# A two-layer gated network on one core: the first stage's normalisation moved to ScalarE, merge units issued in pairs, and one batch's projections started in another PSUM bank

## The chip, the core and the metric

The kernel runs on one core of a Trainium2 chip. The metric is the device time of one execution in microseconds (us), as the median of several runs; lower is better. All tensors are float32 unless a part says bf16. The engines are TensorE (PE in the profile; PEld is its weight load), VectorE (DVE), ScalarE (ACT), GpSimd (POOL) and SyncE (SP, which here only issues DMAs). Each engine works through its own list in order; between engines there are only counted semaphores.

## What is computed

The input `x` is 32 batches of 112 rows by 256 columns, `ctx` is 32 batches of 375 rows by 512 columns. Four blocks are added to `x` one after the other, each with a gate `tanh(g)` and each on a layer-normalised `x`:

```
x = x + tanh(g_xattn[0]) * L0_xattn(layernorm(x), ctx, mask)   # stage 1
x = x + tanh(g_ffn[0])   * L0_ffn(layernorm(x))                 # stage 2
x = x + tanh(g_xattn[1]) * L1_xattn(layernorm(x), ctx)          # stage 3
x = x + tanh(g_ffn[1])   * L1_ffn(layernorm(x))                 # stage 4
```

Stage 1: `x` is RMS-normalised and multiplied by `W_in` plus `b_in`; to it comes a decaying sum over the first rows of the RMS-normalised `ctx`, with weights `exp(-dt * distance)` where the distance comes from a running count over the mask. Stage 2: a hidden layer gives each batch eight gate values; the weights of both matrices of an MLP (256 to 1024 to 256) are merged per batch as `W + sum_e g[b, e] * TW[e]`; the MLP is then run with them. Stage 3: attention with 16 heads of 16 columns over the 375 rows of `ctx` and the 112 rows of `x`, with products of float32 quality made out of bf16 parts. Stage 4: a gated column MLP with a softmax, and a last layer norm.

## The kernel before

**Stage 1** (`stage1`, lines 192 to 478). SP loads the mask, constants, four copies of the `b_in` row (line 260) and then `x` and `ctx` in eight groups of four batches (lines 263, 264). DVE turns the mask into indices and compares them with a row of numbers in one instruction for all batches (`hit`, line 337: output bf16, inputs float32). PE counts the hits (96 products with one column each, line 438), sums them up (line 443) and spreads the result over 32 products (line 447) into eight banks. DVE evacuates the distances in two halves (line 351) and scales them (`distances`, line 300, the first half before the batches, the second during batch 9). ACT squares the rows of `ctx` (line 398). For each half of 16 batches DVE and ACT make the inverse roots together (`inverses`: ACT's root at line 404, DVE's steps at lines 101 to 105).

Then come the 32 batches, in rings of four buffers. For batch b: DVE normalises (`front`, line 361, issued two batches ahead); PE transposes (`turn`, line 458); ACT takes one exponential (line 417) and evacuates the transposed x (line 419); POOL scales the `ctx` rows (line 279) and multiplies them by `g_init` (line 282); PE makes four products with `w_in` (line 468) and two with the exponentials and the rows of `u` (line 471; a float32 product is two instructions); DVE adds the result to the residual (line 367) and takes its statistics (lines 370 and 383). Between the batches DVE also takes the statistics of later groups of `x` (lines 291 and 294).

**Stage 2** (`stage2`, lines 481 to 840). DVE forms the variances of all 32 batches, ACT their roots, DVE the inverses (lines 101 to 105), and only then does `norm` (line 110) give PE something to transpose (line 750). After the gates come eight chunks of the hidden width. A merge unit is four pairs of products with 64 rows of contraction each (`merge_unit`, line 792), after which DVE adds the base weights in two instructions (line 641). A chunk has two phases. In the first, for each of eight groups of four batches: one merge unit for the second matrix, then 16 instructions of the first product (line 815; all 128 rows). In the second, for each two pairs of batches: one merge unit for the first matrix of the next chunk, then 8 instructions of the second product (line 832; 128 rows), whose result DVE adds to the residual (`added`, line 660). Merge results go to two pairs of banks in turn, so unit n waits for DVE's work on unit n-2; the second product's results go to two banks in turn, so pair p waits for `added` of p-2. The last chunk has no second-phase units.

```
for g in range(NG):                     # PE, first phase of a chunk, before
    merge2(c, g)
    ... 16 products of group g ...
```

POOL meanwhile splits the keys of `ctx` into three bf16 parts and stores them to DRAM.

**Stage 3** (`stage3`). A schedule written out by hand over turns -4 to 33 sets the order on each engine; `at(b, operation)` issues the part of batch b that belongs to a turn. A batch is prepared two turns before its scores: `norm` (DVE), `turn_x` (PE, line 1232), `evacuate_x` (ACT, line 1031), `queries_keys` (PE, line 1239), `first_part` (ACT, line 1039), `split` (DVE, line 1159), the parts (POOL, lines 978 to 988), four groups of transposes `turn_parts` (PE, line 1265), evacuated by ACT (keys, line 1054) and DVE (queries, line 1182), and `later_queries` (ACT, line 1064). All of these use one bank, PREP. Then `scores_by_query` (PE, line 1283) and `maximum` (DVE, line 1169) find the row maxima; `scores` (line 1309) and `outputs` (line 1323) follow. For the first batches there is extra work: POOL clears the pads of three rings of buffers (lines 958 to 962) and puts head markers into them (`place_heads`, line 995); ACT does this for the first ring (line 1024); DVE takes the statistics of batches 8 to 31 in three blocks of eight (`late_statistics`, lines 1132 and 1135), the last one between the two evacuations of the first batch's queries.

## Time and profile before

| | |
|---|---|
| median of 3 runs | 1434.84 us (1430.89 to 1436.14) |
| the profiled execution's own time | 1429.99 us |
| its span from the first to the last instruction | 1428.2 us, 32631 instructions |
| mean granted TensorE clock | 0.969 of full speed |
| PE, DVE, ACT, POOL busy | 1324.7, 981.9, 665.4, 558.0 us |

The stages in this execution: stage 1 ends at about 121 us, stage 2 at about 560 us, stage 3 at about 1150 us, stage 4 at 1428 us. How to read the rows below: a time of start and a duration are in microseconds; "x16" is the number of like instructions taken together; in brackets stands how long the engine had been idle before, and what ended that. Matmuls overlap each other's ends, so the distance of two starts tells their pace and the duration does not. The granted clock is 1.00 at 2.4 GHz and 0.50 at 1.2 GHz.

### The profile page before, as it was taken

The numbers are of one execution on the slowest core, as the hardware profiler recorded it, in microseconds if no ns is written. First come the engines' busy times: TensorE is split into PE (matmuls) and PEld (weight loads), VectorE is DVE, ScalarE is ACT, GpSimd is POOL, SyncE is SP. The second block draws the span as 40 slices with busy tenths as digits, with TensorE's granted clock in tenths as the row PEclk, the third lists the DMA queues.
The fourth block names the chain that finished last, engine by engine and source line by source line (L and its number), as shares of the span: only waits on it lengthen the run. The fifth ranks groups of instructions, "written<-read, shape, count | busy, mean of one in ns | idle before, by whom it ended". The sixth has DMA issues, their size and how long they took to land. (4 is left out here: it accounts for less than half of the span.)

```text
span 1428.2 us, 32631 instructions
## 1 busy us (share of the span) xinstructions
PE 1324.7 (93%) x12672; PEld 923.5 (65%) x12672; DVE 981.9 (69%) x1646; ACT 665.4 (47%) x1436; POOL 558.0 (39%) x831
## 2 busy tenths in 40 slices
PE   3687999999999997699999999999999799999997
PEld 2455577777777775367766676766776574555555
DVE  6767656765676567588888888888887554445444
ACT  4433322112112212478878787787877554122221
POOL 0566888888882002533232332323331183000000
PEclk9989999999999999599999999999999799999998
DMA  8404354545451202955566655566552000000000
GB/s 230 107 1 137 98 170 133 161 137 164 137 162 64 66 1 46 174 88 89 89 104 104 100 89 89 98 103 101 95 89 34 2 1 0 14 14 13 26 13 26
DMA packets 92773, 120.25 MB, mean 84 GB/s; under 512 B 7414, under 2 KB 78899, under 8 KB 90348
## 3 DMA queue, kind: packets, MB, share of 16 engines
q1 hardware_dynamic: 83436, 87.82, 30.9%
q0 software_dynamic: 9216, 30.73, 7.7%
q8 instruction: 86, 1.41, 0.4%
q14 instruction: 35, 0.29, 0.1%
HBM read 96.42 MB, written 22.10 MB: 83 GB/s over the span
## 5 line engine op out<-in xcount | busy, mean ns | idle before, releaser
L1169 DVE TENSOR_REDUCE s_neg_max<-banks 112x3 bf16<-112x1461 f32 (+1 forms) x192 | 290.2, 1511 | 45.2 <-PE banks L1283 44.6
L1085 ACT ACTIVATE s_prob<-banks 128x448 f32<-128x448 f32 x512 | 272.4, 544 | 91.8 <-PE banks L1309 76.9
L641 DVE TENSOR_TENSOR s_m<-banks,s_base 128x512 f32<-128x512 f32 x256 | 164.7, 686 | 128.4 <-PE banks L792 128.3
L1309 PE MATMUL banks<-s_q_t,s_k_t 112*128 112x112 bf16 x2048 | 186.6, 215 | 1.1 <-ACT s_prob L1085 1.0
L1309 PEld LDWEIGHTS banks<-s_q_t,s_k_t 112*128 112x128 bf16 x2048 | 124.3, 98 | 72.8 <-issue 50.0
L792 PE MATMUL banks<-s_gate_sel,s_tw 64*128 64x256 f32 x1024 | 146.7, 406 | 1.0 <-DVE s_m L641 0.8
L815 PEld LDWEIGHTS banks<-s_x_t,s_m 128*128 128x128 f32 x1024 | 119.1, 191 | 21.4 <-issue 20.9
L815 PE MATMUL banks<-s_x_t,s_m 128*128 128x112 f32 x1024 | 130.5, 280 | 0.1
L832 PE MATMUL banks<-s_m,s_act_t 128*112 128x256 f32 x512 | 128.5, 388 | 0.6
L1323 PE MATMUL banks<-s_prob,s_v 128*32 128x112 f32 (+1 forms) x4096 | 125.7, 263 | 0.7 <-ACT s_prob L1085 0.7
L732 ACT ACTIVATE s_act_t<-banks,s_bias 128x112 f32<-128x112 f32 x256 | 69.6, 354 | 98.9 <-PE banks L815 98.8
L1801 PE MATMUL banks<-s_proj,s_weighted 128*112 128x256 f32 x512 | 115.4, 380 | 0.0
L792 PEld LDWEIGHTS banks<-s_gate_sel,s_tw 64*128 64x128 f32 x1024 | 89.4, 188 | 36.9 <-issue 20.6
L1801 PEld LDWEIGHTS banks<-s_proj,s_weighted 128*112 128x112 f32 x512 | 90.3, 177 | 28.3 <-issue 10.5
L832 PEld LDWEIGHTS banks<-s_m,s_act_t 128*112 128x112 f32 x512 | 83.4, 176 | 34.9 <-issue 13.9
L732 ACT ACT_TABLE_LOAD x8 | 10.3, 1283 | 202.1 <-PE banks L815 202.1
L1323 PEld LDWEIGHTS banks<-s_prob,s_v 128*32 128x32 f32 (+1 forms) x4096 | 94.6, 110 | 12.4 <-ACT s_prob L1085 1.0
L660 DVE SCALAR_TENSOR_TENSOR x_res<-banks,gates,x_res 112x512 f32<-112x512 f32 x128 | 93.3, 746 | 5.0 <-PE banks L832 4.3
L978 POOL CAST s_qk<-s_rest 112x512 bf16<-112x512 f32 x32 | 19.6, 613 | 176.5 <-DVE s_rest L1159 176.5
L968 POOL COPY s_v<-s_v_raw 128x768 f32<-128x768 f32 x32 | 26.3, 822 | 154.2 <-PE banks L1323 154.2
L1795 PE MATMUL banks<-s_x_t,s_w_cols 128*128 x192 | 85.0, 565 | 0.0
L1283 PE MATMUL banks<-s_k_t,s_q_t 32*112 32x487 bf16 x192 | 79.7, 415 | 4.9 <-DVE s_neg_max L1169 3.7
(270 smaller groups left out, 2311.6 us busy)
## 6 DMA issues: line engine op xcount, KB each, us to landing
k_parts<-s_k_split POOLq DMA_DIRECT2D x64, 281.2 KB, 3.7
s_k_t<-k_parts SPq DMA_DIRECT2D x32, 562.5 KB, 8.0
s_tw<-in_tw SPq DMA_DIRECT2D x16, 1024.0 KB, 5.0
s_k_raw<-in_ctx_k POOLq DMA_DIRECT2D x64, 187.5 KB, 3.8
s_k_t<-k_parts SPq DMA_DIRECT2D x32, 375.0 KB, 5.4
s_v_raw<-in_ctx SPq DMA_DIRECT2D x32, 256.0 KB
s_src<-in_ctx SPq DMA_DIRECT2D x8, 896.0 KB, 15.4
s_k_t<-k_parts SPq DMA_DIRECT2D x32, 187.5 KB, 9.2
```

Source lines behind the costliest of these rows:

```text
L641: nc.vector.tensor_tensor(dst[:, :, :, rows_], got, base[:, :, rows_].unsqueeze(2).broadcast_to([P, 2, B, HR]), ALU.add).then_inc(S["merge ...
L660: nc.vector.scalar_tensor_tensor(out=w.x_res[:, 2 * p:2 * p + 2, :], in0=w.bank(6 + p % 2, T).rearrange("t (b d) -> t b d", b=2), scalar=w ...
L732: last = nc.scalar.activation(act_t[:, b, :], w.bank(4 + g % 2)[:, r * T:(r + 1) * T], ACT.Gelu_apprx_tanh, bias=bias1[:, c, b, :])
L792: last = nc.tensor.matmul(w.bank(2 * (n[1] % 2) + half)[:, m * B * HR:(m + 1) * B * HR], rows_(m)[tile], sel[tile], start=True, stop=True)
L815: last = nc.tensor.matmul(w.bank(4 + g % 2)[:, r * T:(r + 1) * T], m1[:, kk, b, :], x_t[:, kk, b * T:(b + 1) * T], start=(kk == 0), stop=( ...
L832: last = nc.tensor.matmul(y, act_t[:, b, :], m2[:, b, :], start=not first, stop=True)
L1085: nc.scalar.activation(prob[t % 2][:, c, :], w.bank(SCORE + n % SRING, P, TILE), ACT.Exp, scale=DH ** -0.5).then_inc(S["exp_done"], 1)
L1169: nc.vector.tensor_reduce(neg_max[half][:, ROWS + first:ROWS + end, 0], w.banks[0:T, MAX:MAX + end - first, 0:NKEY], AX.X, ALU.max, negate ...
L1309: last = nc.tensor.matmul(w.bank(SCORE + n % SRING)[:, s * T:(s + 1) * T], k_t[k][0:ROWS_MAX, h, c * P:(c + 1) * P], q_t[k][0:ROWS_MAX, h, :],
L1323: last = nc.tensor.matmul(w.banks[s * SLOT:(s + 1) * SLOT, OUT, t * T:(t + 1) * T], v[k][0:K_OF[c], c, t * HS + s, :], prob[t % 2][0:K_OF[ ...
L1795: last = nc.tensor.matmul(w.bank(j % 2, P, GT), w_cols[:, kk, j * P:(j + 1) * P], x_t[:, kk, bass.ds(g * GT, GT)], start=(kk == 0), stop=( ...
L1801: last = nc.tensor.matmul(w.bank(4 + r, T, D), weighted[k][:, j, r * T:(r + 1) * T], proj[:, j, :], start=(j == 0), stop=(j == J4 - 1))
```

## The change

In stage 1 the normalisation goes from DVE (`tensor_scalar`) to ACT (`Identity` with a scale and a bias per row, the bias being `-mean * inverse`). The `hit` comparison is done in bf16 and in four quarters, each awaited by PE on its own. The inverse roots are made in quarters of eight batches instead of halves, so three of four now fall between batches. The second half's distances are evacuated by ACT; the exponentials are taken in place for four batches at once before batch 0 (first half) and before batch 2 (second half). POOL multiplies the `ctx` rows by `g_init` in place and scales the exponentials instead of the rows, in groups of four batches. The `b_in` rows come with one DMA as a 113th row of `src`. PE runs two batches ahead with `turn`. The inverse roots that stage 2 needs for batches 0 to 23 are made at the end of stage 1 (`next_roots`).

```diff
-                nc.vector.tensor_tensor(
-                    hit[:], iota[0:CHUNK, 0:T]....broadcast_to([CHUNK, NQ * B, T]),
-                    idx_t[:]....broadcast_to([CHUNK, NQ * B, T]), ALU.is_equal).then_inc(S["hit_done"], 1)
+                for q in range(Q):
+                    at = slice(q * QB, (q + 1) * QB)
+                    nc.vector.tensor_tensor(
+                        hit[:, :, at, :], iota16[0:CHUNK]....broadcast_to([CHUNK, NQ, QB, T]),
+                        idx_t[:, :, at].unsqueeze(3).broadcast_to([CHUNK, NQ, QB, T]), ALU.is_equal).then_inc(S["hit_done"], 1)
...
+                inverses(0)
+                evacuate_distances()
                 distances(0)
-                inverses(0)
...
+                wait(dve, "evac1", 1)
+                distances(1)
                 for b in range(B):
-                    if b == HB - 2:
-                        inverses(1)
-                    if b + 2 < B:
-                        front(b + 2)
                     last = back(b)
...
+                    if b < 3:
+                        chain.link(x_statistics(QB + 3 * b, min(QB + 3 * b + 3, HB)))
+                    elif b < 11:
+                        chain.link(x_statistics(HB + b - 3, HB + b - 2))
+                    elif b < 19:
+                        chain.link(x_statistics(HB + b - 3, HB + b - 2))
+                    if b in (2, 11, 19):
+                        inverses((b + 6) // 8)
+                    if b == 26:
+                        next_roots()
```

ScalarE's list of stage 1 after the change, after the squares of batches 0 to 7 and their root:

```diff
+                for b in range(QB, QB + GB):
+                    square(b)
+                for b in range(3):
+                    front(b)
+                wait(act, "init_done", 2)
+                wait(act, "spread", 2)
+                wait(act, "rows_done", 2)
+                nc.scalar.activation(expo[0:T, HB * T:B * T]..., w.banks[0:T, HG:NG, 0:GT],
+                                     ACT.Identity, bias=offset[0:T]).then_inc(S["evac1"], 1)
+                exps(0)
+                for b in range(2):
+                    evacuate_x(b)
+                front(3)
+                for b in range(QB + GB, HB):
+                    square(b)
+                exps(1)
+                for b in range(2, B):
+                    if b == 4:
                         roots(1)
+                    if b == 13:
+                        roots(2)
+                    if b == 21:
+                        roots(3)
+                    if b == 28:
+                        ... root for stage 2 ...
+                    evacuate_x(b)
+                    if b + 2 < B:
+                        front(b + 2)
+                    if 4 <= b < 20:
+                        square(HB + b - 4)
```

PE and POOL of stage 1:

```diff
-                    wait(pe, "m_done", b + 1)
-                    wait(pe, "u_done", b + 1)
-                    nc.tensor.matmul(y, m_scan[0:T + 1, r, :], u[0:T + 1, r, :], start=False, stop=True)\
+                    wait(pe, "scaled", b // GB + 1)
+                    wait(pe, "u_done", b // GB + 1)
+                    nc.tensor.matmul(y, expo[0:T + 1, b * T:(b + 1) * T], src[0:T + 1, b, 0:D], start=False, stop=True)\
...
                 turn(0)
+                turn(1)
+                wait(pe, "evac1", 1)
+                pe.wait_ge(bias_in, 16)
                 for b in range(B):
-                    if b + 1 < B:
-                        turn(b + 1)
+                    if b + 2 < B:
+                        turn(b + 2)
                     product(b)
```

In stage 2 two merge units follow each other in both phases, and `norm(0)` and `norm(1)` come before the roots of the last eight batches:

```diff
                     for g in range(NG):
-                        merge2(c, g)
+                        if g % 2 == 0:
+                            merge2(c, g)
+                            merge2(c, g + 1)
...
                     for p in range(PAIRS):
-                        if p % 2 == 0 and not final:
+                        if p % 4 == 0 and not final:
                             merge1(c + 1, p // 2)
+                            merge1(c + 1, p // 2 + 1)
...
-                    for p in range(PAIRS):
-                        if p % 2 == 0:
-                            merged1(c + 1, p // 2)
+                    for p in range(0, PAIRS, 4):
+                        merged1(c + 1, p // 2)
                         added(c, p)
+                        added(c, p + 1)
+                        merged1(c + 1, p // 2 + 1)
+                        added(c, p + 2)
+                        added(c, p + 3)
```

In stage 3 batch 1 is transposed and projected in the bank OUT before the first batch's parts are transposed; POOL clears the second and third ring later; ACT places the first ring's heads in two halves; DVE takes the late statistics of 16 batches in one block after the first `split`:

```diff
+        def prep(b):
+            return OUT if b == 1 else PREP
...
+                    if b == 0:
+                        clear(1)
                     if b < 2:
                         place_heads(b + 1)
+                    if b == 0:
+                        clear(2)
...
                     if b == 0:
-                        place_heads()
+                        evacuate_x(1)
+                        place_heads(0)
...
                     if b == 0:
-                        late_statistics(2 * EARLY, 3 * EARLY)
+                        late_statistics(2 * EARLY, B)
+                        variances(EARLY, B)
...
                 def turn_parts(b, n):
 
+                    if (b, n) == (0, 0):
+                        turn_x(1)
+                        for kk in range(KD):
+                            queries_keys(1, kk)
...
                         if b < RING:
-                            pe.wait_ge(rows_ready[k], 2)
+                            pe.wait_ge(rows_ready[k], 2 if k else 3)
...
                         wait(pe, "v_done", b + 1)
+                        if b == 0:
+                            wait(pe, "rest_done", 2)
```

## Rows read from the trace of the kernel before

**Rows 1.** Window of stage 1: length, PE, PEld, DVE, ACT, POOL busy, clock, DMA, GB/s:

```profile
62.00:77.00 15.00, 11.97 (x45) 8.68 (x43) 10.68 (x37) 6.52 (x24) 7.85 (x10) 0.77 0.00 1
```

**Rows 2.** Timeline, the head of stage 1 and one bf16 copy of stage 2:

```profile
12.16 11.36 DVE L337 TENSOR_TENSOR s_hit<-s_iota,s_idx_t 125x10752 bf16<-125x10752 f32 x1
23.58 9.12 PE L438 MATMUL banks<-s_ones,s_hit 125*112 125x1 bf16 x96 [13.88 <-DVE s_hit L337]
...
36.92 4.20 DVE L351 TENSOR_SCALAR s_expo<-banks,s_iota 112x1792 f32<-112x1792 f32 x2 [0.17 <-PE banks L447]
...
46.53 2.05 PE L468 MATMUL banks<-s_w_in,s_x_t 128*112 128x256 f32 x4
...
134.28 2.08 DVE L614 COPY s_batch_of<-s_ident 96x3584 bf16<-96x3584 bf16 x1
```

**Rows 3.** Timeline of PE, the start of one batch and of the next:

```profile
97.59 0.36 PE L458 MATMUL banks<-ident,s_xn 112*128 112x112 f32 x2
...
99.08 0.37 PE L458 MATMUL banks<-ident,s_xn 112*128 112x112 f32 x2
```

**Rows 4.** Groups of instructions by form, 0 to 125 us (busy us, mean ns | idle before):

```profile
L282 POOL TENSOR_TENSOR s_u<-s_src,s_g_init 112x256 f32<-112x256 f32 x32 | 25.1, 785 | 2.7
L398 ACT ACTIVATE s_squares<-s_src 112x512 f32<-112x512 f32 x32 | 19.8, 619 | 14.2 <-DMA s_src<-in_ctx 14.2
L361 DVE TENSOR_SCALAR s_xn<-x_res,mean_var,s_inv 112x256 f32<-112x256 f32 x32 | 16.5, 521 | 0.2
L370 DVE BATCH_NORM_STATS2 s_stats<-x_res 112x6 f32<-112x256 f32 x32 | 13.7, 427 | 1.1
L419 ACT ACTIVATE s_x_t<-banks 128x224 f32<-128x224 f32 x32 | 11.4, 356 | 40.3 <-PE banks L458 40.3
L404 ACT ACT_TABLE_LOAD x2 | 2.6, 1283 | 0.0
```

**Rows 5.** Timeline, the last work of stage 1 and PE's first of stage 2:

```profile
121.08 0.38 DVE L383 BATCH_NORM_AGGREGATE mean_var<-s_stats 112x2 f32<-112x6 f32 x4
...
126.18 3.22 PE L750 MATMUL banks<-ident,s_act_t 112*128 112x112 f32 x16 [6.06 <-DVE s_act_t L110]
```

**Rows 6.** Timeline of PE in a first phase; shorter windows show parts of the same runs:

```profile
279.71 2.04 PE L815 MATMUL banks<-s_x_t,s_m 128*128 128x112 f32 x16
281.68 1.13 PE L792 MATMUL banks<-s_gate_sel,s_tw 64*128 64x256 f32 x8
282.74 2.04 PE L815 MATMUL banks<-s_x_t,s_m 128*128 128x112 f32 x16
...
280.13 1.61 PE L815 MATMUL banks<-s_x_t,s_m 128*128 128x112 f32 x13
...
282.21 0.60 PE L792 MATMUL banks<-s_gate_sel,s_tw 64*128 64x256 f32 x4
...
282.43 0.38 PE L792 MATMUL banks<-s_gate_sel,s_tw 64*128 64x256 f32 x2
```

**Rows 7.** Timeline of DVE in a second phase, one unit and the next:

```profile
256.03 1.29 DVE L641 TENSOR_TENSOR s_m<-banks,s_base 128x512 f32<-128x512 f32 x2 [1.74 <-PE banks L792]
...
259.00 1.29 DVE L641 TENSOR_TENSOR s_m<-banks,s_base 128x512 f32<-128x512 f32 x2 [0.32 <-PE banks L792]
```

**Rows 8.** Timeline and one line's account (starts of L958) at the head of stage 3:

```profile
L958 POOL MEMSET s_k_t<- x3: 306/311/312, 564.5 to 568.2; 112x256 bf16 x3
...
579.22 2.70 DVE L1132 BATCH_NORM_STATS2 s_late_stats<-x_res 112x6 f32<-112x256 f32 x8
...
579.36 0.93 PE L1265 MATMUL banks<-s_ident,s_qk 112*128 112x112 bf16 x8 [0.72 <-DVE s_q_t L1182]
...
584.51 1.36 ACT L1064 ACTIVATE s_q_odd<-s_q_t 32x448 bf16<-32x448 bf16 x2
...
588.95 0.41 PE L1283 MATMUL banks<-s_k_t,s_q_t 32*112 32x487 bf16 x1
...
589.58 0.61 POOL L978 CAST s_qk<-s_rest 112x512 bf16<-112x512 f32 x1 [7.52 <-DVE s_rest L1159]
```

More of the change, by code:

```diff
@@ L57 @@
 EARLY = 8
+READY = 24
 def nth(n):
@@ L397, in square, with roots @@
                     wait(act, "squared", b - 1)
[L398 removed]
+                    nc.scalar.activation(squares[:, b % 2, :], src[0:T, b, :], ACT.Square,
                                          accum_out=total[:, b:b + 1]).then_inc(S["squared"], 1)
[L401 to L403 removed]
+                def roots(q):
+                    at = slice(q * QB, (q + 1) * QB)
+                    wait(act, "ms_done", q + 1)
@@ L404, in roots, with front, exps @@
                     nc.scalar.activation(root[:, :, at], ms[:, :, at], ACT.Sqrt).then_inc(S["root_done"], 1)
-                for b in range(HB):
+                def front(b):
+                    wait(act, "inv_done", b // QB + 1)
+                    wait(act, "x_tr", b - U + 1)
+                    nc.scalar.activation(xn[:, b % U, :], w.x_res[:, b, :], ACT.Identity, bias=shift[:, b, :],
+                                         scale=inv[:, 1, b, :]).then_inc(S["xn_done"], 1)
+                def exps(half):
+                    wait(act, "expo_done", half + 1)
+                    for g in range(half * HG, (half + 1) * HG):
+                        at = slice(g * GT, (g + 1) * GT)
+                        nc.scalar.activation(expo[0:T, at], expo[0:T, at], ACT.Exp, scale=-dt).then_inc(S["exp_done"], 1)
@@ L407, in _, with evacuate_x @@
+                def evacuate_x(b):
+                    r = b % U
+                    wait(act, "x_tr", b + 1)
+                    wait(act, "y_done", b - U + 1)
+                    nc.scalar.activation(x_t[:, r, :, :], w.bank(r, P, KD * T).rearrange("p (k t) -> p k t", k=KD),
+                                         ACT.Copy).then_inc(S["x_t_done"], 1)
+                for b in range(QB):
                     square(b)
                 roots(0)
-                nc.scalar.activation(table[:], w.gates[:, 0:1], ACT.Exp)
@@ L598, in norm @@
                         normalised(nc, w, xn[:, b % (2 * GB), :], b).then_inc(S["xn_done"], 1)
+                norm(0)
+                norm(1)
+                dve.wait_ge(S["root_done"], 1)
+                chain.link(inverse_root(nc, chain, w.rstd[:, late, 0], root[:, late], var[:, late], tmp[:, late]))
+                chain.link(nc.vector.tensor_copy(ident16[:], w.ident[0:3 * B, 0:3 * B]))
+                chain.link(nc.vector.tensor_tensor(ident16[:, 0:B], ident16[:, 0:B], ident16[:, B:2 * B], ALU.add))
+                chain.link(nc.vector.tensor_tensor(ident16[:, 0:B], ident16[:, 0:B], ident16[:, 2 * B:3 * B], ALU.add))
                 def sums(i):
```

223 lines of the change are left out of this document (105 added, 118 removed).

## The prediction

> **What bounds the kernel now.** I read the page first, for its slices of busy time: PE is nearly full from stage 2 on, and the slices that are not full are the head of stage 1, its batches, and the seams before stages 2, 3 and 4. The change touches the first three of these and the body of stage 2. Then I read each of those places in the timeline.
>
> Stage 1's batches: in a stretch of 15 us PE is busy 11.97, DVE 10.68, and the granted clock is 0.77, a mix of its two levels 1.2 and 2.4 GHz [rows 1]. Neither engine is full: PE waits for the normalised x, which DVE makes between its other duties. Where PE doesn't wait, one batch takes 99.08 - 97.59 = 1.49 us [rows 3], so 32 batches could take 47.7 us. They take from 46.53 to 121.46, 74.9 us [rows 2, 5]. The head before them is one chain through DVE: 11.36 us of comparison, 9.12 us of counting on PE, then statistics, evacuations, roots [rows 2].
>
> Stage 2's body is bound by PE, but not at one pace throughout. In the run of products of line 815 starts are (1.61 - 0.28) / 12 = 0.111 us apart, taking 0.28 as the length of one, so 16 of them need 1.78 us; yet the merge unit starts 281.68 - 279.71 = 1.97 us after them. In the unit the pairs are 282.43 - 282.21 = 0.22 apart (0.216 in the finer reading), four need 0.86, yet the next group starts 1.06 us later [rows 6]. So each unit that stands between groups costs 0.19 + 0.20 = 0.39 us beyond its work, at its entry and its exit, where the 64-row form gives way to the 128-row form. In the second phase the period is 259.00 - 256.03 = 2.97 us, of which DVE is idle 0.32 only [rows 7].
>
> **The change part by part.** The sums are made against the profiled execution, 1429.99 us, whose span is 1428.2; the median of the runs is 4.85 us above it, which is added at the end.
>
> **Head of stage 1.** The comparison keeps 10752 elements per partition. It ran at 11.36 / 10.752 = 1.06 ns each with float32 inputs; a bf16 copy that reads each element many times over ran at 2.08 / 3.584 = 0.58 ns [rows 2]. No row has the two-input operation with bf16 alone, so it is bounded by 11.4 and 6.2 us. I take 11.4, because the row of the same operation is nearer than that of a copy. The Trainium skill, "Vector Engine (DVE) Microarchitecture Reference", section 5.1, reports a two-source operation with 2-byte operands, one of them one element read again and again, at one element per tick; this speaks against the quicker figure. By that rule the sum stays as it is here, by the copy's pace the rival below holds.
>
> The counting now starts after a quarter. Its last quarter alone stays behind the comparison: 9.12 x 3/4 = 6.8 us gained; with the quick comparison PE's 9.12 us would be the limit and 9.8 would be gained. Behind the counting, the statistics of two of the four groups go (four passes of 0.427 us each and the aggregates, some 1.9 a group; one of them is only moved ahead of the counting's end, so I count 1.9 twice at most) and one of two evacuations moves to ACT, 4.20 / 2 = 2.1 us [rows 2, 4]: 5.9. Added there are a table load, 1.28, and four exponentials of 448 columns that all stand before the first evacuation of x: 4 x 0.54, scaled from the 0.619 of 512 columns [rows 4], 2.2 us: 3.5 against. Net 2.4. POOL's first scaling runs beside these exponentials. ACT's new fill of the bias rows stands in ACT's idle time before the first squares. SP issues one small DMA in place of four ahead of the inputs; I count nothing. Head: 6.8 + 2.4 = 9.2 us, products starting at 37.3 instead of 46.53.
>
> **Batches of stage 1.** DVE loses 16.5 us of normalising [rows 4]. ACT then has per batch an evacuation (0.356), a normalisation (0.356 to 0.619, by its two neighbours; I take 0.4) and for 16 batches a square (0.619) [rows 4]: 1.4 at most beside PE's 1.49, so it is hidden, but thinly. POOL per four batches: 1024 elements at up to 4 x 0.785 and 448 at up to 1.4, 4.5 us beside 6.0, hidden [rows 4]. DVE keeps an add, a pass of statistics and, for 19 batches, one to three more passes at 0.427; about 1.5, level with PE.
>
> The three later quarters of inverse roots and `next_roots` are new meeting points. DVE asks for the root after its add of batch b and stops until ACT gives it; ACT has stopped before its evacuation of b + 2; PE can finish one more product and then lacks a normalised x. Behind ACT's wait stand its evacuation and `front`; behind DVE's wait the next add and PE's ring of results. From the add (0.43) through one or more passes (0.43 each), the root, the evacuation (0.36) and the normalisation (0.4) it is about 2 to 3.5 us after a product, of which PE covers 1.49. Bounds: 0 and 3.3 each. I take 2, four times: 8 us. A clock that starts low costs 1.5 us for each of two batches, and I take 2 us more for falls after those waits: 5 us. With 1.6 us from the last product to the last aggregate: 47.7 + 8 + 5 + 1.6 = 62.3 us, from 74.9: 12.6 us gained. The end of stage 1 is then 121.5 - 9.2 - 12.6 = 99.7.
>
> **Seam to stage 2.** From the end of stage 1 to PE's first transpose are 126.18 - 121.46 = 4.7 us [rows 5], most of it root and inverse. For batches 0 to 23 these now exist, so `norm` starts after the variance. I take 3.0; bounds 2 and 4. The work that was ahead of `norm` comes after eight of them, beside PE's eight transposes and first hidden products.
>
> **Body of stage 2.** Eight first phases and seven second phases lose four entries and exits each: 60 x 0.39 = 23.4 us, or 22.6 with 0.377 by the finer reading; I take 22.6. The first phase has nothing in the way: DVE only does 1.29 us per unit there. In the second phase DVE needs 2 x (2.97 - 0.32) = 5.30 us for two units and four results, and PE's period falls from 5.94 to 5.56. DVE's second unit now stands between results whose bank PE waits for: tracing the order by these durations, PE comes 0.1 to 0.25 us late per period, 28 periods. I take 0.18: 5 us given back. Net 17.6 (12.1 of it in the first phases, bounds 12 and 22.6 in all).
>
> **Head of stage 3.** The first batch's maxima wait for the second query evacuation, which stood behind DVE's 2.70 us of statistics that began at 579.22 [rows 8]. Without it the queries are out 2.4 us earlier, about 0.6 us after PE's last transposes end at 580.29; the copies of the odd queries (1.36) follow, and `scores_by_query` starts near 582.4 instead of 588.95, since the second batch's projections no longer stand before it [rows 8]. DVE's `split` of that batch comes before the first maximum, so the gain there is 6.0. POOL had been idle 7.52 us when it got that split, at 582.06, and now has two clearings of (568.2 - 564.5) / 2 = 1.85 us moved behind the first batch's parts [rows 8]; if the earlier start doesn't make up for them, it is ready at 585.8 and the gain is 3.8. SP's loads are issued as before. I take 5.5, bounds 3.7 and 6.5. The body of stage 3 and stage 4 I cost at nothing: no instruction of theirs changes.
>
> Sum: 9.2 + 12.6 + 3.0 + 17.6 + 5.5 = 47.9 us. 1429.99 - 47.9 = 1382.1; plus 4.85 is 1387.
>
> **The rivals.**
>
> A. Stage 1 stays starved. The four meeting points and a ScalarE at 1.4 of 1.49 us keep PE pausing, and the clock stays where it was, 0.77 [rows 1]. 47.7 / 0.77 = 62 us instead of 47.7 + 5 adds 9 us, waits of 3.3 instead of 2 add 5: 1387 + 14 = 1401. For it: in the old run gaps of this size went with the low clock. Against it: in the new order they come at four places and not at every second batch. Chance 0.15.
>
> B. The pairs don't save what the switch seems to cost: half of the 0.39 us belongs to the head of a unit (its first weights are loaded only after the wait) and stays with each unit. Then 60 x 0.19 = 11.4 less 5 remains: 1387 + 11 = 1398. Against it: the group after a unit pays too, and has no such head of its own. Chance 0.12.
>
> C. The comparison runs at the copy's pace: the head gains 3.0 us more, 1384. Chance 0.12.
>
> D. Slower than before: in second phases PE waits for DVE at every fourth result, long enough for the clock to be low half the time (0.75), as the pauses of stage 1 did. These phases last 7 x 23.8 = 166 us; at 0.75 they take 55 us more, and 5 more are lost to waits: 1387 + 60 = 1447. It decides where PE pauses there as it does in rows 1; at a full clock it would take waits of (48 + 7) / 28 = 2 us a period to end slower. By the durations above the wait is 0.1 to 0.25. Chance 0.03.
>
> **How the numbers follow.** The forecast as summed has 0.58, and 1387 is its time. Its own range, with waits of 0.5 to 3 us per meeting point and the bounds of the other parts, is 1376 to 1398. The range takes in A and B nearly whole and C below: 1372 to 1403. About 0.5% (7 us) is what a measurement of this kernel can tell from no change. All cases but D and unforeseen ones are faster by more: 0.96; within 0.5% 0.01; slower 0.03.
>
> **What the new profile would show.** The comparison as four instructions of 2.8 us (C: 1.5), counting that ends some 2.5 us after them, first products of line 468's kind near 37 us, their batches 1.5 us apart with four gaps, stage 1 over near 100 us. Merge runs of 16 instructions followed by 32, with a period of 5.68 us (from 6.06) in first phases, and between 5.6 and 5.8 in second ones. In stage 3 the first `scores_by_query` 6 us nearer to the stage's start. I am wrong if the gaps in stage 1 come with every batch, if the pairs' periods stay near 6.0, or if POOL's clearings put the second batch's parts later than now.

## The result, and the profile after

The kernel after takes 1385.91 us (median of 4 runs, 1383.04 to 1387.77) against 1432.87 for the kernel before; the ratio is 0.968 (0.963 to 0.972). The forecast was 1387 us. A second set of runs of the same kernel gave 1386.74 us and 0.969 (0.966 to 0.971). The profiled execution took 1387.4 us with a span of 1385.6. In the kernel before, stage 4's first instruction on DVE starts at 1127.09 us; the 1150 given ahead of the prediction was too high.

From the page of the kernel after, busy time by engine:

```profile
PE 1304.1 (94%) x12672; PEld 924.2 (67%) x12672; DVE 968.4 (70%) x1641; ACT 678.4 (49%) x1447; POOL 528.1 (38%) x781
```

The windows of its stages: start and end, length, busy time of PE, PEld, DVE, ACT, POOL (with counts), granted clock, DMA share, GB/s. The first row is stage 1's batches, the second stage 2, the third stage 3, the last two stage 4:

```profile
37.59:98.02 60.43, 52.43 (x250) 40.57 (x250) 46.66 (x174) 39.25 (x109) 19.82 (x13) 0.97 0.25 60
99.69:517.74 418.05, 410.81 (x2746) 318.55 (x2746) 281.38 (x463) 100.05 (x316) 266.95 (x385) 0.99 0.41 122
517.74:1080.09 562.35, 535.59 (x8384) 370.09 (x8384) 467.39 (x608) 426.18 (x807) 187.18 (x311) 0.97 0.58 95
1080.09:1107.40 27.31, 24.66 (x94) 18.48 (x95) 15.28 (x50) 11.79 (x41) 16.80 (x22) 0.51 0.00 1
1107.40:1385.60 278.20, 265.00 (x1061) 162.42 (x1059) 129.99 (x298) 77.30 (x133) 29.81 (x43) 0.99 0.04 14
```

The timeline, head of stage 1 to PE's first work of stage 2:

```profile
11.71 11.56 DVE L367 TENSOR_TENSOR s_hit<-s_iota,s_idx_t 125x2688 bf16<-125x2688 bf16 x4
23.33 2.40 PE L494 MATMUL banks<-s_ones,s_hit 125*112 125x1 bf16 x24 [0.47 <-DVE s_hit L367]
34.03 1.28 ACT L438 ACT_TABLE_LOAD   x1
35.33 1.98 ACT L438 ACTIVATE s_expo<-s_expo 112x448 f32<-112x448 f32 x4
37.59 2.04 PE L524 MATMUL banks<-s_w_in,s_x_t 128*112 128x256 f32 x4 [2.89 <-ACT s_x_t L444]
...
43.37 0.42 PE L514 MATMUL banks<-ident,s_xn 112*128 112x112 f32 x2 [0.53 <-ACT s_xn L431]
48.74 0.49 PE L514 MATMUL banks<-ident,s_xn 112*128 112x112 f32 x2 [2.17 <-ACT s_xn L431]
66.11 0.41 PE L514 MATMUL banks<-ident,s_xn 112*128 112x112 f32 x2 [2.03 <-ACT s_xn L431]
79.66 0.41 PE L514 MATMUL banks<-ident,s_xn 112*128 112x112 f32 x2 [1.39 <-ACT s_xn L431]
90.88 0.41 PE L514 MATMUL banks<-ident,s_xn 112*128 112x112 f32 x2 [0.55 <-ACT s_xn L431]
...
97.64 0.38 DVE L396 BATCH_NORM_AGGREGATE mean_var<-s_stats 112x2 f32<-112x6 f32 x4
...
99.69 3.10 PE L814 MATMUL banks<-ident,s_act_t 112*128 112x112 f32 x16 [3.00 <-DVE s_act_t L111]
```

The first product comes at 37.59 instead of 46.53 [rows 2]. Of the counting only the last quarter stands behind the comparison. In the batches PE has five waits for the normalised x, 6.7 us in all, and the clock over all of them is 0.97. The 0.77 of [rows 1] was that of a low stretch; over all the batches of the kernel before it was 0.91:

```profile
46.53:121.46 74.93, 60.26 (x252) 43.47 (x252) 52.68 (x165) 29.06 (x97) 53.48 (x63) 0.91 0.04 10
```

So PE's idle time fell from 14.7 to 8.0 us, and its busy time from 60.3 to 52.4. From DVE's last aggregate to PE's first transposition are 1.67 us, formerly 4.7 [rows 5].

PE in stage 2, a first phase and a second one, and DVE at a second phase's results:

```profile
248.63 3.83 PE L881 MATMUL banks<-s_x_t,s_m 128*128 128x112 f32 x32
252.38 2.00 PE L856 MATMUL banks<-s_gate_sel,s_tw 64*128 64x256 f32 x16
...
225.24 4.01 PE L899 MATMUL banks<-s_m,s_act_t 128*112 128x256 f32 x16
229.17 2.00 PE L856 MATMUL banks<-s_gate_sel,s_tw 64*128 64x256 f32 x16
231.10 4.01 PE L899 MATMUL banks<-s_m,s_act_t 128*112 128x256 f32 x16
...
232.26 1.61 DVE L721 SCALAR_TENSOR_TENSOR x_res<-banks,gates,x_res 112x512 f32<-112x512 f32 x2 [0.54 <-PE banks L899]
```

These are the pairs: 16 merge matmuls, then 32 of a first phase, or 16 of a second one. A period is the time from one such pair to the next. The first phase's next 32 start at 254.31, a period of 5.68 us as forecast; the second phase's period is 231.10 - 225.24 = 5.86, where 5.74 was forecast. DVE idles 0.54 us ahead of the first result of a four, while PE is late too: neither engine is full.

The head of stage 3, where a row appears that the kernel before has not:

```profile
531.96 5.18 POOL L1072 CAST s_k_t<-ident 16x6000 bf16<-16x6000 f32 x1
532.86 4.31 DVE L1201 TENSOR_SCALAR s_var<-mean_var 112x24 f32<-112x24 f32 x1
537.08 1.65 DVE L111 TENSOR_SCALAR s_xn<-x_res,mean_var,rstd 112x256 f32<-112x256 f32 x1
538.65 0.60 DVE L1264 COPY s_q_t<-banks 128x896 bf16<-128x896 bf16 x1
539.32 0.93 PE L1349 MATMUL banks<-s_ident,s_qk 112*128 112x112 bf16 x8 [5.99 <-DVE s_q_t L1264]
...
542.55 0.62 PE L1367 MATMUL banks<-s_k_t,s_q_t 32*112 32x487 bf16 x1 [0.51 <-ACT s_q_odd L1144]
```

An addition over 24 elements takes 4.31 us and ends with POOL's copy (532.86 + 4.31 = 537.17, 531.96 + 5.18 = 537.14). PE stands 5.99 us for the query evacuation behind it.

**Where the time went**, by stage, in us. The second column compares the two profiled executions. The third takes the mean over all traces of this study that run the same code in that stage (three of the old code, five to seven of the new), since single traces differ by their low-clock stretches:

| part | forecast | the two profiles | mean of traces |
|---|---|---|---|
| head of stage 1 | 9.2 | 8.9 | 46.3 to 37.4: 8.9 |
| its batches | 12.6 | 14.5 | 73.2 to 61.0: 12.2 |
| seam to stage 2 | 3.0 | 3.1 | 3.1 |
| stage 2 | 17.6 | 16.7 | 434.8 to 418.5: 16.3 |
| stage 3 | 5.5 | 3.8 | 565.8 to 562.6: 3.2 |
| stage 4 (no edit) | 0 | -4.4 | not compared: 298.1 to 305.5 over all traces |
| sum | 47.9 | 42.6 | 43.7 |

By the medians the gain is 47.0 us (1432.87 to 1385.91), and 44.7 in the second set, beside the kernel before run with it (1431.48 to 1386.74).

### The profile page after: what moved, and what is told of

Read it like the earlier page. It is cut to its first block and busy times, and to the rows that moved or that the text cites. A ratio compares the mean times of both kernels' runs of the same rounds, so it can differ in the third digit from the quotient of the medians.

```text
span 1385.6 us, 32665 instructions
## 1 busy us (share of the span) xinstructions
PE 1304.1 (94%) x12672; PEld 924.2 (67%) x12672; DVE 968.4 (70%) x1641; ACT 678.4 (49%) x1447; POOL 528.1 (38%) x781
## 5 line engine op out<-in xcount | busy, mean ns | idle before, releaser
L702 DVE TENSOR_TENSOR s_m<-banks,s_base 128x512 f32<-128x512 f32 x256 | 161.1, 683 | 99.2 <-PE banks L856 98.9
L856 PE MATMUL banks<-s_gate_sel,s_tw 64*128 64x256 f32 x1024 | 130.8, 394 | 1.6 <-DVE s_m L702 1.5
L881 PE MATMUL banks<-s_x_t,s_m 128*128 128x112 f32 x1024 | 122.4, 278 | 0.0
L856 PEld LDWEIGHTS banks<-s_gate_sel,s_tw 64*128 64x128 f32 x1024 | 94.7, 189 | 27.4 <-issue 9.7
L1638 ACT ACTIVATE s_hid_c<-banks,s_b_cols 128x448 f32<-128x448 f32 x48 | 30.3, 633 | 112.9 <-PE banks L1884 112.5
```

Source lines behind the costliest of these rows:

```text
L702: nc.vector.tensor_tensor(dst[:, :, :, rows_], got, base[:, :, rows_].unsqueeze(2).broadcast_to([P, 2, B, HR]), ALU.add).then_inc(S["merge ...
L856: last = nc.tensor.matmul(w.bank(2 * (n[1] % 2) + half)[:, m * B * HR:(m + 1) * B * HR], rows_(m)[tile], sel[tile], start=True, stop=True)
L881: last = nc.tensor.matmul(w.bank(4 + g % 2)[:, r * T:(r + 1) * T], m1[:, kk, b, :], x_t[:, kk, b * T:(b + 1) * T], start=(kk == 0), stop=( ...
```

## The experiments

**The three stages one at a time.** Each takes the kernel before and exchanges one stage.

The new stage 1 alone:

```diff
(in words)
-stage1 of before, b_in_row
+stage1 of after, b_in_rows    (stage 2 as before, with all roots of its own)
```

> The kernel before with the new stage 1 alone; stage 2 still computes all its inverse roots itself, so the seam keeps its 4.7 us. My theory: the first product at 37.6 us instead of 46.5 and the last aggregate at 98.0 instead of 121.5, so 23.4 us off stage 1, about 1409 against 1433, and nothing given back in stages 2 to 4. Rival (the end of stage 1 is not what stage 2 waits for, because loads or POOL's splitting hold it): less than 15 us, with a longer gap before stage 2's first transpose.

Measured: 1406.3 us, ratio 0.984 (0.982 to 0.987), 20.6 us below the kernel before as it ran beside it. First product at 37.51, last aggregate at 98.00, as in the kernel after. Stage 2 takes 434.6 us, as before. The seam is 4.0 us, not the 4.7 expected. So in the trace the gain of stage 1 arrives whole; the rival (something else holds stage 2) falls.

The pairs alone:

```diff
-                        merge2(c, g)
+                        if g % 2 == 0:
+                            merge2(c, g)
+                            merge2(c, g + 1)
...
-                        if p % 2 == 0 and not final:
+                        if p % 4 == 0 and not final:
                             merge1(c + 1, p // 2)
+                            merge1(c + 1, p // 2 + 1)
```

> The kernel before with the merge units in twos alone, in both phases of a chunk. My theory: eight first phases at a period of 5.68 us for each two groups instead of 6.06 give 12.1 us, seven second phases at 5.86 instead of 5.94 give 2.4, and the first phase pays 1.7 us at the start of each chunk's pass only where ten units stand ahead of the first group (once): 13 us in all, about 1420 against 1433. Rival as I predicted it: second phases at 5.74, 17.6 us. Rival B: half of the entry and exit cost stays with each unit, 6 us or less.

Measured: 1412.4 us, ratio 0.989 (0.987 to 0.991), 14.5 us. In the trace stage 2 falls from 434.75 to 419.15, by 15.6: more than the 13 I then expected, less than the 17.6 forecast. From the first group to the start of PE's last product it falls by 16.8 (378.53 to 361.69); at its head, where ten units and not nine stand before the first group, it grows by 1.2 (54.19 to 55.43). Rival B (6 us or less for the pairs by this run's expectation) falls.

Pairs in first phases only, on the kernel after:

```diff
-                    for p in range(0, PAIRS, 4):
-                        merged1(c + 1, p // 2)
-                        added(c, p)
...
+                    for p in range(PAIRS):
+                        if p % 2 == 0:
+                            merged1(c + 1, p // 2)
+                        added(c, p)
```

> The kernel after with pairs of merge units in the first phases only; the second phases keep one unit ahead of every two results, as before. My theory from the periods: second phases return to 5.94 us from 5.86, 28 of them, so 2.4 us slower than after (1388 against 1386) although 28 entries and exits of 0.38 us come back (10.6 us if they had been saved in full); the period of the first phase stays at 5.68. By the prediction's figure (0.18 us of wait per period) it would be 5.6 us slower.

Measured: 1391.6 us, ratio 0.973 (0.970 to 0.975). From the first group to the last result 365.41 us against 361.72. So the pairs of the second phases are worth 3.7 us, those of the first phases 13.1. That lies between my two figures (2.4, 5.6): the first left out that in the first chunk, whose results are longer, the pairs save more (a period of 6.45 us against 6.76). The rest of the difference to the kernel after lies outside: stage 2's head is 1.7 us longer here (56.0 against 54.3), and as long in the repeated run of the kernel after (56.05). Over that head the clock is 0.91 in the first profile of the kernel after, 0.89 here and 0.88 in the repeated one.

The new stage 3 alone:

```diff
(in words)
-stage3 of before
+stage3 of after
```

> The kernel before with the new stage 3 alone. My theory: the first transposition of the maxima comes 2.6 us earlier after the stage's start and the second batch's 3.3 us, whole stage about 3.5 us shorter, near 1429 against 1433; the trace again shows DVE's addition of 24 variances at over 4 us, ending as POOL's 5.2 us copy of the heads' rows ends. As predicted it would have been 5.5 us, with that addition at 0.2 us.

Measured: 1423.1 us, ratio 0.995 (0.993 to 0.998). The transposition of the maxima comes 31.91 us after the stage's start (34.5 before), the stage lasts 563.1. The time is 3.8 us below the kernel before run beside it. DVE and POOL in its timeline:

```profile
571.79 5.18 POOL L1005 CAST s_k_t<-ident 16x6000 bf16<-16x6000 f32 x1
...
572.69 4.32 DVE L1134 TENSOR_SCALAR s_var<-mean_var 112x24 f32<-112x24 f32 x1
```

The long addition is there without the other parts.

**What holds the addition.** POOL's copies of the heads' rows go behind the second and third batch's parts, with the clearing ahead of each; DVE's order stays.

```diff
-                    if b == 0:
-                        clear(1)
                     if b < 2:
-                        place_heads(b + 1)
-                    if b == 0:
-                        clear(2)
+                        clear(b + 1)
+                    if b in (1, 2):
+                        place_heads(b)
...
-                    wait(pool, "q_parts_done", k)
+                    wait(pool, "q_parts_done", k + 1)
```

> The kernel after, with POOL's 5.2 us copies of the heads' rows moved behind the second and third batch's parts (and the clearings after them); DVE's order is untouched. My theory: DVE's addition of 24 variances and its normalisation are held by that copy, nothing else. Then they take 0.2 and 0.4 us instead of 4.31 and 1.65, the query evacuations come some 4 to 5 us earlier, the first scores by query near 26 us after the stage's start instead of 31.9 for the transposition of the maxima (27 for that), and the stage is 4 to 5 us shorter: 1381 against 1386. Rival (the addition waits for something of DVE's own, such as the aggregates before it): it still takes over 4 us and the head of the stage is unchanged.

DVE's and POOL's timeline of this kernel:

```profile
533.01 0.18 DVE L1199 TENSOR_SCALAR s_var<-mean_var 112x24 f32<-112x24 f32 x1
533.10 0.92 DVE L111 TENSOR_SCALAR s_xn<-x_res,mean_var,rstd 112x256 f32<-112x256 f32 x1
533.94 0.61 DVE L1262 COPY s_q_t<-banks 128x896 bf16<-128x896 bf16 x1
...
544.58 5.18 POOL L1070 CAST s_k_t<-ident 16x6000 bf16<-16x6000 f32 x1
549.84 0.72 POOL L1078 TENSOR_TENSOR x_res<-x_res,s_b_proj 112x256 f32<-112x256 f32 x1
550.51 0.82 POOL L1041 COPY s_v<-s_v_raw 128x768 f32<-128x768 f32 x1
...
548.78 0.62 DVE L1262 COPY s_q_t<-banks 128x896 bf16<-128x896 bf16 x1
549.85 1.52 DVE L104 TENSOR_TENSOR s_tmp<-s_tmp,s_var 112x24 f32<-112x24 f32 x1
```

The addition is back at 0.18 us with nothing changed on DVE: the copy held it. (The 0.92 of the normalisation stands beside another POOL copy, 533.01 to 533.87; with POOL idle, in the kernel with all three edits below, it is 0.41.) The transposition of the maxima comes at 27.06 us, 4.85 earlier, and the first product of `outputs` at 40.79, 2.5 earlier. In this profile the stage is 4.0 us shorter (558.4), for which the copy need not be the whole cause. The time is 1383.3 us, ratio 0.968 (0.966 to 0.971), which by itself shows no gain over the kernel after. In the three later kernels with this edit the transposition comes at 26.4, 27.0 and 27.0 us, and yet the stage lasts 562.4, 560.5 and 562.0. The last 30 us of the stage, first in this kernel, then in the one with all three edits:

```profile
1046.26:1076.26 30.00, 22.37 (x404) 15.72 (x404) 15.39 (x24) 16.07 (x33) 0.00 (x0) 0.99 0.01 2
1039.91:1069.91 30.00, 22.62 (x359) 16.11 (x357) 13.79 (x22) 15.16 (x31) 0.00 (x0) 0.90 0.01 2
```

The clock is 0.99 in the one and 0.90 in the other (0.96 in the kernel after). So the earlier head is shown in four traces, a shorter stage in one; what sets the clock at the stage's end stays open. The last row of the timeline above shows the holding again elsewhere: a product over 24 elements takes 1.52 us beside two POOL instructions, and ends as the second does. Beside the same 5.18 us copy DVE's copy out of PSUM keeps its 0.62.

**What the second phases wait for.** Results in a ring of four banks:

```diff
+    RESULTS = (6, 7, 4, 5)
...
-in0=w.bank(6 + p % 2, T)
+in0=w.bank(RESULTS[p % 4], T)
...
-pe.wait_ge(S["act_done"], nth(NG * c + p // 2))
-pe.wait_ge(S["x_done"], nth(PAIRS * c + p - 2))
+pe.wait_ge(S["act_done"], nth(NG * c + (p + 4 if p in (2, 3) else p // 2)))
+pe.wait_ge(S["x_done"], nth(PAIRS * c + p - 4))
...
+                        if g < 2:
+                            pe.wait_ge(S["x_done"], nth(PAIRS * c - 2 + g))
```

> The kernel after, with the second phase's results in a ring of four banks (the two of the first phase's groups, idle by then, and their own two) instead of two. My theory: in second phases PE waits 0.3 us in each period for DVE to free one of two result banks, not for lack of DVE's time (5.3 us of work in a period of 5.86). With four banks the period is 5.56 us and seven chunks gain 7 to 8.4 us: about 1378 against 1386. Rival (DVE is full there, or PE's own switch is the 0.3): the period stays at 5.86 and nothing is gained.

PE's timeline, then DVE's:

```profile
225.08 3.71 PE L902 MATMUL banks<-s_m,s_act_t 128*112 128x256 f32 x16
228.71 2.00 PE L857 MATMUL banks<-s_gate_sel,s_tw 64*128 64x256 f32 x16
230.64 3.71 PE L902 MATMUL banks<-s_m,s_act_t 128*112 128x256 f32 x16
...
231.80 1.62 DVE L722 SCALAR_TENSOR_TENSOR x_res<-banks,gates,x_res 112x512 f32<-112x512 f32 x2 [0.24 <-PE banks L902]
```

The period is 5.56 us. Sixteen results take 3.71 us and not 4.01, and DVE idles 0.24 a period, formerly 0.54. From the first group to the start of PE's last product: 352.67 us against 361.72, 9.05 less (2.2 of it in the last chunk, which has no merging); stage 2 as a whole goes from 418.05 to 410.10, 7.95 less. In the first chunk, whose results are longer, almost nothing is gained (6.45 to 6.42 a period). The time is 1373.4 us, ratio 0.960 (0.958 to 0.962). That is 12 to 13 us below the kernel after, more than stage 2 explains; the profiled execution, at 1379.1, was the slowest of the five, and the rest stays open. From the second chunk on the wait was for a bank, not for DVE's time.

**What stage 1's waits are.** First the meeting points are taken apart:

```diff
-                    if b in (2, 11, 19):
-                        inverses((b + 6) // 8)
+                    if b in (2, 10, 18):
+                        variances(b // 8 + 1)
+                    if b in (3, 11, 19):
+                        inverses(b // 8 + 1)
...
                     evacuate_x(b)
                     if b + 2 < B:
                         front(b + 2)
+                    if b in (5, 13, 21):
+                        roots(b // 8 + 1)
```

> The kernel after, with each meeting point of stage 1 taken apart: DVE posts the variances at batches 2, 10, 18 and 24 and goes on, ScalarE takes the roots behind its normalisation of three batches later, DVE inverts them one batch after it posted them. My theory: PE's waits for the normalised x, 6.7 us in all, come from the meeting points and fall to about 2, so stage 1 ends near 93.5 us instead of 98.0 and the kernel takes 1381 against 1386. Rival (ScalarE is too full at 1.4 us of 1.49 a batch, whatever the order): the waits move to other batches and less than 1.5 us is gained.

Measured: 1377.6 us, ratio 0.963 (0.961 to 0.966), but the batches take 58.8 us against 60.4. PE's waits are 0.31, 2.11, 1.39 and 1.24: 5.05 us, not 2. My theory falls. The time is nevertheless 8 to 9 us below the kernel after, and the ranges don't meet: its five executions took 1376.1 to 1379.5, the ten of the kernel after 1380.8 to 1389.1. Of that, 1.6 us is in the batches; 7.4 is in stage 4, 298.1 us in this profile and 305.5 in that of the kernel after, with one code. The granted clock of these five is 0.974 to 0.977. The executions of the kernel after and of its float32 twin (below) that reach 0.975 or 0.976 took 1379.8 to 1380.8, so at a like clock 0 to 4 us are left. Whether the edit brings the shorter low-clock stretch in stage 4 was not tested. ScalarE stood 1.98 us for the shift, and DVE had its statistics ahead of the inversion.

The three edits together:

```diff
(in words)
+    the ring of four, the heads' rows later, the meeting points apart
```

> All three edits together on the kernel after: the ring of four banks, the heads' rows later, the meeting points taken apart. They lie in three different stages, so if each does what its own run says, the gains add: 7.5 + 4.5 + 4.5 = 16.5 us, about 1369 against 1386. A rival is the clock: its low stretches at the heads of stages 3 and 4 lasted 24 and 27 us in the kernel after; if a stage that starts earlier gets a longer one, 3 to 5 us are given back.

Measured: 1370.5 us, ratio 0.958 (0.956 to 0.961), where 1369 was expected. The sum fits, its parts don't: stage 2 takes 411.2 us and the batches 57.8 (at a clock of 1.00), but stage 3 takes 562.4, so its 4.5 us are missing. Then the inversion directly behind the batch's own statistics:

```diff
                         chain.link(last)
+                        if b in (3, 11, 19):
+                            inverses(b // 8 + 1)
                         for r in range(U):
```

> The three edits together once more, with one move in stage 1: DVE's inversion of the roots at batches 3, 11 and 19 goes ahead of the aggregates and the next statistics, directly behind the batch's own pass of statistics. Theory from the run of the parted meeting points: DVE, level with PE in these batches, has 0.6 to 1.0 us of aggregates and statistics queued before the inversion, and ScalarE stood 2.0 us for the shift; so PE's waits (2.47, 1.69, 1.25 us in the combined kernel) each fall by 0.6 to 1.0, stage 1 ends 2 to 3 us earlier and the kernel takes 1368 against 1370.5. Rival: ScalarE itself is late by the table load and the 0.6 us normalisation; then the three waits stay above 1.2 us.

Measured: 1371.0 us, ratio 0.959 (0.956 to 0.961), no gain. PE in the timeline:

```profile
50.99 0.41 PE L522 MATMUL banks<-ident,s_xn 112*128 112x112 f32 x2 [1.49 <-ACT s_xn L443]
64.83 0.41 PE L522 MATMUL banks<-ident,s_xn 112*128 112x112 f32 x2 [1.68 <-ACT s_xn L443]
78.68 0.41 PE L522 MATMUL banks<-ident,s_xn 112*128 112x112 f32 x2 [1.68 <-ACT s_xn L443]
```

In the combined kernel before it these waits were 2.47, 1.69 and 1.25: the first fell, the second stayed and the third rose, 0.56 us less in all. The place of the inversion in DVE's queue is not the main cause. DVE's additions before them start at 58.87 and 60.33 us, 1.46 apart and without idle time, beside PE's 1.49 a batch; a quarter's eight further instructions take 1.4 us by their starts (0.15 for the variances, 1.21 for the inversion and shift), near what PE waits. So DVE's load comes under test. This kernel leaves out the statistics of the second half's inputs, so its results are wrong and only its time counts:

```diff
-                        chain.link(x_statistics(HB + b - 3, HB + b - 2))
+                        dve.wait_ge(src_in[(HB + b - 3) // GB], 32)
+                        chain.link(nc.vector.bn_aggr(w.mean_var[:, HB + b - 3, :], stats[:, 0, :]))
```

> The previous combined kernel without DVE's 16 passes of statistics (0.41 us each) over the second half's inputs in batches 3 to 18; the aggregates stay and read batch 0's statistics, so the second half is normalised with wrong numbers and only the time counts. The passes for batches 8 to 15 stay. Theory: DVE has no time to spare in these batches (1.47 us of work and hand-overs in 1.49), so each inversion of 1.3 us with its two variances comes out as a wait of PE of 1.5 to 1.7 us. With 0.4 us a batch to spare it is made up: PE's waits before batches 16 and 24 fall from 1.68 to under 0.8 us each, the first one, behind the three passes a batch that stay, keeps about 1.5. Rival: the hand-overs themselves (variance, root, inversion, normalisation, transposition) are too long for their place in the order, whatever DVE's load; then the waits before batches 16 and 24 stay above 1.2 us.

PE's timeline of this kernel:

```profile
49.54 0.41 PE L521 MATMUL banks<-ident,s_xn 112*128 112x112 f32 x2 [0.74 <-ACT s_xn L442]
62.16 0.41 PE L521 MATMUL banks<-ident,s_xn 112*128 112x112 f32 x2 [0.46 <-ACT s_xn L442]
74.79 0.41 PE L521 MATMUL banks<-ident,s_xn 112*128 112x112 f32 x2 [0.46 <-ACT s_xn L442]
```

The waits before batches 16 and 24 fall to 0.46 each, the batches from 57.3 to 54.1 us. The first wait falls too, to 0.74, where I expected 1.5; why it did stays open. The time of 1369.8 us (ratio 0.957, 0.954 to 0.960) shows little of it: stage 3 takes 562.0 us here and 560.5 in the kernel before it. With 0.4 us a batch to spare DVE makes up the inversion; what remains of the waits I put down to the hand-overs, without a run of its own.

**The comparison's type:**

```diff
-        idx_t = sb("s1_idx_t", [CHUNK, NQ, B], BF16)
+        idx_t = sb("s1_idx_t", [CHUNK, NQ, B])
...
-hit[:, :, at, :], iota16[0:CHUNK]
+hit[:, :, at, :], iota[0:CHUNK, 0:T]
```

> The kernel after with float32 inputs to the comparison (output still bf16). Theory: the element read again and again sets the pace, not the type; each quarter takes 2.87 us as with bf16, 1.07 ns per element, and the kernel is unchanged at 1386. Rival (bf16 inputs did help): the quarters take longer than 2.87 us and the first product comes later than 37.6.

DVE's timeline of this kernel:

```profile
11.55 11.56 DVE L367 TENSOR_TENSOR s_hit<-s_iota,s_idx_t 125x2688 bf16<-125x2688 f32 x4
```

The same 11.56 us for four quarters; 1383.8 us, ratio 0.967 (0.964 to 0.970). The bf16 inputs bring nothing.

**The kernel after, repeated:**

> The kernel after once more, unchanged, beside the next two on their chip: 1386 us. Its stretches at the low clock at the heads of stages 3 and 4 lasted 24 and 27 us in the first profile; if their length is a matter of chance from run to run, the length of stage 4 here may be anything between 298 and 306 us with the same instructions; if it belongs to the kernel, it is 305.5 again.

Measured: 1386.7 us. Stage 4 lasted 300.5 us in this profile, 305.5 in the first: with one kernel the length varies from execution to execution.

## Why the prediction was right, and where it was off

It was right: 1387 forecast, 1385.9 measured, each of the five terms within 2.3 us by the mean of the traces. That the two agree to 1 us is luck. The terms were forecast at 47.9 us in all and sum to 43.7 by the traces, most of them too high; and the kernel before, taken as 1434.84 us from three runs, is 1432.87 with a fourth. 1432.87 - 43.7 would be 1389. The 3 us between that and the 1385.9 I can't attribute; one stage without any edit varied by more than that between traces.

**Head of stage 1**: 9.2 forecast, 8.9 measured. The comparison ran at 1.08 ns an element (11.56 / 10.752), near the 1.06 that I had taken from [rows 2], and rival C is refuted. The Trainium skill's "Vector Engine (DVE) Microarchitecture Reference", section 5.1, says so of a two-source operation with 2-byte operands and one element read again and again; the trace agrees, and the float32 run shows that the type of the inputs makes no difference to this comparison. The four exponentials took 1.98 us (2.2 forecast), the table load 1.28.

**Batches**: 12.6 forecast, 12.2 by the mean. PE's busy time was to be 47.7 + 5 = 52.7 us and is 52.4; the rest, 8 for four meeting points and 1.6 at the end, was to be 9.6 and is 8.0, of which 6.7 are PE's waits. The reason given for the waits was off. I had written that DVE "stops until ACT gives it", and took ScalarE's margin to be the thin one. The two runs that removed the stops and moved the inversion gained 1.6 and 0.5 us in the batches; the run that took load off DVE cut two of the waits from 1.68 to 0.46. In batches 3 to 18 DVE has no time to spare, so what a quarter adds to its queue comes out at PE. Rival A (starved throughout, clock 0.77) is refuted by 0.97; its 0.77 held for one stretch even before.

**Seam**: 3.0 forecast, 3.1 measured.

**Body of stage 2**: 17.6 forecast, 16.3. The entries and exits of [rows 6] were read rightly: first phases at 5.68 us. Two terms were mis-sized. The pairs of the first phases gave 13.1 us where 12.1 was counted. (The 0.377 us of an entry and an exit isn't worked out in the prediction, whose rows give 0.39; 6.06 - 5.68 = 0.38 bears it out.) For the second phases I took a wait of 0.18 us a period; it was 0.3, and their pairs gave 3.7 us instead of 5.5. I had counted DVE's work (5.30 us in 5.56) and put down the lateness to the order; the ring of four shows that it was the two banks. The tenth unit at the head of the stage was not in the sum; the head grew by 1.2 us with the pairs alone. Rival B falls with the pairs' 15.6 us in stage 2, D with a second phase's period that fell and a clock of 1.00 from the first group to the last result.

**Head of stage 3**: 5.5 forecast, 3.2 measured, below my bound of 3.7. The failed step is that, without the 2.70 us of statistics between the evacuations [rows 8], "the queries are out 2.4 us earlier". The second evacuation of the queries starts 22.54 us after the stage's start, formerly 21.81, so 0.7 later. The statistics were moved up with the addition of the variances, and that fell beside POOL's 5.2 us copy. I had followed POOL's queue for when its results come and not for what it takes from DVE. `scores_by_query` starts 3.2 us nearer to the stage's start and not 6 (28.04 to 24.81), and POOL's parts of the second batch come 2.7 us earlier (28.67 to 25.97), where 3.8 was the least I allowed. With the copy out of the way the second evacuation starts at 17.69, and the transposition of the maxima is 7.5 us earlier than before (34.5 to 27.06).

**Stage 4 and the clock.** Stage 4 has no edit, and its length ran from 298.1 to 305.5 us. It goes with the stretch at the low clock at its beginning. The window of its first 60 us in the first profile of the kernel after:

```profile
1080.05:1140.05 60.00, 56.65 (x309) 42.93 (x310) 32.02 (x86) 30.68 (x89) 35.62 (x48) 0.77 0.00 1
```

And in the profile of its repetition:

```profile
1084.03:1144.03 60.00, 56.64 (x322) 40.26 (x322) 34.08 (x88) 33.05 (x92) 38.43 (x53) 0.86 0.00 1
```

The clock is 0.77 in the first and 0.86 in the second, and the stage is 5.0 us longer in the first. I counted nothing for it, and this is more than any of my errors. What decides the length of that stretch no run here shows.

## What to carry to other kernels

Where a small form of matmul stands between large ones, read the distance of starts across the change of form; grouping the small ones saved it in full here where nothing else was late (0.38 us for an entry and an exit). Before costing a wait by its hand-over, add up the queue of the engine that must serve it: here, with no time to spare, a new duty of 1.4 us cost PE about as much in both places where it was tried, while a wait on one of two buffers went away with four. When work moves on POOL or DVE, lay the two engines' rows side by side: a tiny DVE instruction that ends with a long POOL one may be held by it, and moving the long one shows whether it is. And compare stages, with the clock beside each, before you credit an edit with a difference of a few us in the whole time.

## What the runs showed of the hardware

A DVE addition over 24 float32 elements took 4.31 us beside a POOL copy that reads SBUF, 0.18 without; the normalisation of 256 elements behind it took 1.65 against 0.41; a DVE copy out of PSUM beside the same kind of copy kept 0.62. The sixteen aggregates of DVE's statistics, which overlapped the start of the copy, took 1.17 us with it and without it. In stage 1 of the kernel with fewer statistics DVE and POOL show the holding once more (0.96 us, 0.17 in the kernel before it):

```profile
58.34 0.96 DVE L328 TENSOR_SCALAR s_ms<-s_total 112x8 f32<-112x8 f32 x1
...
56.90 2.36 POOL L277 TENSOR_TENSOR s_src<-s_src,s_g_init 112x1024 f32<-112x1024 f32 x1 [2.11 <-ACT s_squares L430]
```

The trace puts the wait into the instruction's own duration (4.31 us), so it shows as no idle time. The Trainium skill's "SBUF — State Buffer", section "SBUF: two separate sides", describes a port pair shared by the two engines, and calls it an "exclusive lock" and not a bandwidth split, for DVE in its two-port modes, or with two SBUF inputs against a GpSimd operation that reads SBUF. The rows agree, down to the copy from PSUM that is spared at 0.62 us. That the lock is the mechanism is the page's statement; the runs show the holding and its end.
